# Probabilities times values in halves of 375 queries, every second round

## The reference, cut to what matters

```
h = h + attention(layernorm(h))          # 12 heads of 16, low-rank q, k, v
h = h + moe_ffn(layernorm(h))            # 8 experts, the best 2, and a shared one
```

```
attn = softmax(qm @ km * scale, axis=-1)     # 750 queries x 750 keys
out  = attn @ v                              # 750 x 16
```

## Time and profile before

| | |
|---|---|
| median of 3 runs | 3381.99 us (3378.26 to 3388.05) |
| the profiled execution | 3387.41 us, span 3385.6 us |
| mean granted clock of TensorE | 0.96 |
| PE busy | 3120.8 us (92%) |
| DVE busy | 2153.1 us (64%) |
| ACT busy | 1675.6 us (49%) |
| POOL busy | 630.7 us (19%) |
| product of exponentials and values | 9216 matmuls, 584.8 us busy |
| the chain that ended last | PE 70%, DVE 14%, ACT 7% |

### The profile page before, as it was taken

One profiled execution on the slowest core, in us unless ns is written; L12 is line 12 of the kernel. 1 busy time (PEld: TensorE's weight loads), 2 busy tenths in 40 slices (PEclk: granted clock), 3 DMA queues, 4 the chain that ended last, 5 costly groups with the idle time before them and its releaser, 6 DMA issues.

```text
span 3385.6 us, 56227 instructions
## 1 busy us (share of the span) xinstructions
PE 3120.8 (92%) x22512; PEld 1795.2 (53%) x22512; DVE 2153.1 (64%) x3828; ACT 1675.6 (49%) x2419; POOL 630.7 (19%) x1097
## 2 busy tenths in 40 slices
PE   6888999999999999998999999999999999999977
PEld 3543455464555546464554646455554646455545
DVE  3317666766766676676767676676667667667635
ACT  1123654646455464646546464645546464655542
POOL 1520130301212030211203030121303021120211
PEclk7667999999999999999999999999999999999989
DMA  5325220312122031312213031222203131221000
GB/s 128 112 88 106 73 53 14 79 29 72 33 63 45 15 89 23 79 23 70 38 40 72 14 79 26 67 41 59 50 15 80 32 77 24 64 38 28 7 8 7
DMA packets 146212, 174.52 MB, mean 52 GB/s; under 512 B 30081, under 2 KB 134874, under 8 KB 143950
## 3 DMA queue, kind: packets, MB, share of 16 engines
q1 hardware_dynamic: 143772, 163.37, 20.1%
q0 software_dynamic: 1280, 7.08, 0.9%
q10 hardware_dynamic: 898, 0.47, 0.1%
HBM read 105.49 MB, written 64.51 MB: 50 GB/s over the span
## 4 chain that ended last, share of the span: by engine, by line
PE 70%; DVE 14%; ACT 7%; issue 4%; SPq 2%; DMA 2%; POOL 1%; ACTq 0%; DVEq 0%; POOLq 0%
PE ps L1118 67%; DVE negm L929 7%; ACT big L746 2%; DVE st L873 2%; ACT hn L709 1%; PE ps L1204 1%; ACT rest L671 1%; PE ps L1292 1%; ACT parts L687 1%; DVE mpart L936 1%; SPq L384 1%; DVE onrm L960 1%; DVE rest L1033 1%; POOL h0t L494 0%; DVE mvr L879 0%
## 5 line engine op out<-in xcount | busy, mean ns | idle before, releaser
L929 DVE TENSOR_REDUCE negm<-ps 125x1 f32<-125x750 f32 x1152 | 1064.2, 935 | 548.4 <-PE ps L1118 536.4
L746 ACT ACTIVATE big<-ps 125x750 f32<-125x750 f32 x1152 | 907.3, 794 | 659.1 <-PE ps L1118 656.2
L1118 PE MATMUL ps<-qs,ks 99*125 99x375 bf16 x2304 | 615.5, 349 | 69.7 <-DVE negm L929 59.1
L1118 PE MATMUL ps<-ks,qs 96*125 96x375 bf16 x2304 | 587.2, 337 | 64.0 <-ACT big L746 28.7
L1118 PE MATMUL ps<-big,V 125*32 125x188 f32 (+1 forms) x9216 | 584.8, 333 | 3.3 <-ACT big L746 0.4
L1033 DVE SCALAR_TENSOR_TENSOR rest<-ps,fb,h1s 128x375 f32<-128x375 f32 (+1 forms) x448 | 251.7, 603 | 322.9 <-PE ps L1118 321.6
L1118 PEld LDWEIGHTS ps<-qs,ks 99*125 99x125 bf16 x2304 | 230.3, 136 | 402.1 <-issue 223.4
L1118 PEld LDWEIGHTS ps<-ks,qs 96*125 96x125 bf16 x2304 | 292.0, 140 | 209.2 <-issue 52.8
L760 ACT ACTIVATE h1s<-ps,fb,wsc 128x375 f32<-128x375 f32 (+1 forms) x448 | 272.4, 658 | 210.6 <-PE ps L1118 210.6
L494 POOL TENSOR_TENSOR h0t<-h0t,onrm 125x384 f32<-125x384 f32 x48 | 48.1, 1002 | 1751.7 <-DVE onrm L960 1751.7
L1118 PEld LDWEIGHTS ps<-big,V 125*32 125x32 f32 x9216 | 195.9, 108 | 298.9 <-issue 285.2
(11 more groups left out here) (176 smaller groups left out, 3250.3 us busy)
## 6 DMA issues: line engine op xcount, KB each, us to landing
qs<-qk_scratch SPq DMA_DIRECT2D x288, 93.8 KB, 3.5
ks<-qk_scratch SPq DMA_DIRECT2D x288, 93.8 KB, 4.5
qk_scratch<-parts SPq DMA_DIRECT2D x32, 562.5 KB, 4.7
v_scratch<-vtmp SPq DMA_DIRECT2D x16, 1125.0 KB
V<-v_scratch SPq DMA_DIRECT2D x48, 375.0 KB
h_scratch<-h0t SPq DMA_DIRECT2D x16, 562.5 KB
hn<-h_scratch SPq DMA_DIRECT2D x16, 562.5 KB
h0t<-h_scratch SPq DMA_DIRECT2D x16, 562.5 KB
```

What stands on the lines that cost most here:

```text
L746: nc.scalar.activation(halves(probs[:, i % 2, h, :]), slot(s, TP), ACT.Exp).then_inc(exp_done, 1)
L929: V_.tensor_reduce(negm[:, n:n + 1], slot(s, TP), axis=AX.XY, op=MAX, negate=True).then_inc(max_done, 1)
L1118: return nc.tensor.matmul(o, l, r, start=start, stop=stop)
```

## The change

A product part has 375 columns instead of 188 or 187, so a block has two parts and a group 12. Part n of a group stands behind the A tile (or behind the B tile, where a round has no A) of round 4 (n // 2) + 5 + 2 (n % 2), that is of the rounds 5, 7, 9, ..., 23. The two parts of the last block stand behind the A tiles of the next group's first two rounds. Nothing is issued behind the last B tile of a group any more.

```
-PV_COLS = ((0, 188), (188, 375), (375, 563), (563, 750))
-PV_FROM = HG + 1
+PV_COLS = ((0, 375), (375, 750))
+PV_AT = {HG * (n // 2) + HG + 1 + 2 * (n % 2): (n,) for n in range(2 * J - 2)}
+PV_FIRST = {0: (2 * J - 2,), 1: (2 * J - 1,)}
 PV_LAST = range(len(PV_COLS) * (J - 1), len(PV_COLS) * J)
...
-                    if pending is not None and kind in "AB" and k < 2:
-                        if ("A", k) in tiles:
-                            pv_parts(*pending, (PV_LAST[2 * k + (kind == "B")],))
-                        elif kind == "B":
-                            pv_parts(*pending, PV_LAST[2 * k:2 * k + 2])
-                    if kind == ("A" if ("A", k) in tiles else "B") and k > PV_FROM:
-                        if k == PV_FROM + 1:
-                            pv_parts(b, g, (0,))
-                        pv_parts(b, g, (k - PV_FROM,))
+                    if kind == ("A" if ("A", k) in tiles else "B"):
+                        if pending is not None:
+                            pv_parts(*pending, PV_FIRST.get(k, ()))
+                        pv_parts(b, g, PV_AT.get(k, ()))
...
-                pv_parts(b, g, range(TILES - PV_FROM, PV_LAST[0]))
                 if not hold:
                     pv_parts(b, g, PV_LAST)
```

## The result

The median of the kernel after is 3406.23 us (six runs, 3397.77 to 3411.12), that of the kernel before, run beside it, 3379.09 (six runs, 3364.04 to 3388.05). The ratio is 1.0085 with the interval [1.0066, 1.0103]: slower, by 27 us. The forecast was 3408 and slower, by 26.

What follows compares the result with a forecast made beforehand. TensorE's order was taken as the clock wherever nothing else holds it. Losses of 2.0 us a batch over 13 whole batches, edges cancelling, gave +26: 3382.0 + 26 = 3408 us, likeliest 3394 to 3430, 8 in 10 3378 to 3440.

Steps and rivals of the forecast that it cites:

- A waits in each pair: Plain rounds: A waits 0.41 us for ACT to read its slot, so a pair takes 2.65 instead of 2.49.
- The piece of 375 columns: One long V on TensorE takes 0.77 us from its start to the next B.
- The first V: Group start: asked one round earlier, still starts behind DVE's normalisation; two tiles come behind it, price 0.66 us a group.
- Second group: From its first A: pending entries -0.5, first V and nine pairs +1.75, end -0.55; sum +0.7 us.
- Third group: First projection tile P after round six comes 1.0 us later, the remaining rounds come out even; sum +1.0 us.
- First group: Start loses about 0.85 us, mostly regained where DVE and ACT set the time; sum +0.3, at worst +0.9, at best -0.5.
- A batch: Sum of the three groups' losses in a whole batch: 0.7 + 1.0 + 0.3 = 2.0 us.
- The first batch: Edge of the run: the first batch adds about 2 us, the next to last 1.
- The last batch: Edge of the run: -2 us in its final group of B tiles only, -1 in the group before.
- The price of an entry: TensorE: each V standing alone pays about 0.28 us for being entered and left; 31 fewer a batch, 8.7 us.
- the 10 either way: Batches shifting against TensorE's lower clock level: at most 21 us won or lost, 10 us either way held likely.
- named signs: Profile signs: A's idle time behind exponentials well over 100 us, pairs of 2.65, V of 0.77, first group least changed.

Runs made afterwards that it cites:

- The extra tile: A tiles of even rounds 6 to 22 computed twice, in the kernel after (3425.67 us, ratio 1.0114) and in the kernel before (3458.65 us, ratio 1.0216).
- V behind B: The kernel after with V behind the B tile of the same rounds instead of the A tile: 3420.17 us, ratio 1.0136.
- the reader made earlier: Kernel after with first piece in round six, plus the exponential in two instructions of 375 columns where an uncovered A takes the slot: 3339.24 us, ratio 0.9865.

## Why the prediction was right, point by point

- **A waits in each pair.** Forecast 1.42 from B to the A in its slot, 0.41 of it wait, a pair of 2.65; measured 1.42, 0.40 and 2.65. In a second group all nine pairs take 2.65 to 2.71; in seven of them A waits for ACT in nearly every batch, in the other two another wait comes first. The extra tile shows that it is idle time, V behind B that the distance decides which reader is late.
- **The piece of 375 columns.** Forecast 0.77 to the next B; measured 0.77 (1840.78 to 1841.54, and 1827.51 to 1828.28).
- **The first V.** Forecast: no earlier than before, right behind the normalisation, and 1.46 from V to B of round six instead of 0.80. Measured 1827.51 to 1828.98, 1.47. Putting it back gives 2.3 us a batch.
- **Second group.** Forecast +0.7 without the feed-forward part. From the last B of the first group, it was 33.91 (1813.33 to 1847.24) and is 34.62 (1817.95 to 1852.57): +0.71. Its end shrank by 0.54 (0.91 to 0.37), forecast 0.55.
- **Third group.** Forecast +1.0 from the first P on. V to P was 1.17 (1733.47 to 1734.64, from the earlier trace rows) and is 2.19, as the rows below show: +1.02, and the stretch is 1.01 longer.
- **First group.** Forecast +0.3. From A of round 2 to the last B it was 35.46 and is 35.73: +0.27. The stretch shows -0.25, since it ends with the second group's first rounds, whose pending pieces (-0.5) the prediction counts with the second group.
- **A batch.** Forecast 2.0 us, measured 2.00.

The rows of the third group, PE:

```profile
1736.76 0.84 PE L1119 MATMUL ps<-big,V 125*32 125x375 f32 x8 [1.30 <-ACT big L747]
1737.53 0.54 PE L1119 MATMUL ps<-qs,ks 99*125 99x375 bf16 x2
1737.90 0.49 PE L1119 MATMUL ps<-ks,qs 96*125 96x375 bf16 x2
1738.22 0.48 PE L1119 MATMUL ps<-qs,ks 99*125 99x375 bf16 x2
1738.95 0.90 PE L1119 MATMUL ps<-xA,wq 128*128 128x375 f32 x2 [0.24 <-ACT big L747]
```

Some terms were off. The first batch lost 4.4 us, not 2, and the next to last 3.9, not 1: its third group has no P tiles, so all its pairs pay (33.89 became 36.84). Most of what the first batch lost beyond 2.0 lies in its first group, which has no tiles of an earlier feed-forward part: from its first B to its last it went from 29.27 to 30.58, where in a whole batch it went from 38.22 to 37.66, and its rounds from six on are pairs of 2.65 to 2.66 throughout. The last batch gained 2.4, forecast 3. The edges then give +5.9 instead of 0, and with 13 x 2.00 = 26.0 the rounds cost 31.9. The price of an entry, 0.28, does not follow from the rows beside it in the prediction, which give 0.60 - 0.35 = 0.25. With the measured 0.77 of the long piece it comes out all the same: two short pieces alone cost 1.20, one long one 0.42 + 0.77 + 0.05 - 0.32 = 0.92 (the 0.05 is B to A after a V, 0.37, against 0.32).

The clock hid a part of this in the profiled pair. TensorE was at its lower level, granted clock 0.50 or 1.2 GHz, in 11 short stretches of the profiled execution before (behind the front end; ten ahead of the last batch and one in its first group) and in 2 of that after. A third group with one is 1.53 us longer than without (56.36 and 54.83 above; 54.50 and 52.90 in the earlier trace rows). Nine fewer are 13.7 us. With 2.0 less in front end and tail, 31.9 - 13.7 - 2.0 = 16.2, the 16 between the profiled executions. The medians differ by 27, where 31.9 - 2.0 = 29.9 would be due at an equal clock and 26 was forecast: the edges were 6 too low, and the rest lies inside the 10 either way that the prediction held open for the clock. So that 27 came so near to 26 is in part luck: the 2.0 of a batch was right, the edges were not, and the front end with the tail and some 3 us of unknown origin made up for them. How many such stretches the other runs had is not known, and what decides their number was not found: the eight other kernels' profiled executions had between 4 and 11.

One of the named signs was just missed. Idle time before A with the exponential as releaser was to be well over 100 us and is 98.4; the 70.8 of the V pieces stand beside it. And the account of the loss was right in its sum but put its stress on one half: "what I hold decisive" was the V in every second round. Measured, the halves are of one size: the first piece put back gives 2.3 us a batch, and the reader made earlier on top of that another 2.4 (192.66 to 190.29, sums of the stretches). The waits in the pairs use up what the entries save, and what is then lost against before is the price of the first piece asked for one round early.

## What to carry to other kernels

Where few slots go round, count for each tile the time from its start to the start of the tile that takes over its slot, and compare it with the latency of its reader, not with the reader's load: ACT was busy 48% and still made PE wait in most of the plain pairs. Work that is bunched to save switches takes cover away from the gaps it leaves; spread it so that each distance keeps some, or free the slot in pieces, and bunch only then. And before a piece is asked for earlier, see what it waits for: on an in-order engine an early request that can't start is a wall in front of work that could.

## What was unexpected of the hardware

Two halves of an exponential follow each other within 0.38 us, where one of double length takes 0.80: splitting it costs ACT 0.06 in time to the end, and frees the first bank 0.32 earlier (0.48 against 0.80). The number of stretches at the lower clock varies from 2 to 11 among the profiled executions of these ten kernels, one of each and of nearly the same work. At 1.53 us a stretch that moves a time by some 14 us (an estimate); a profile of one execution on either side can't tell changes smaller than that apart, and spans had to be compared by groups with full clock.
